# The second merged stage of a recurrent network kernel: routing by pairs of tiles, and the third LSTM 24 steps behind the second

## The reference, cut to what matters

```
hs = LSTM_1(x, h0=cond)            # second LSTM of the kernel: 128 times, one after the other
# experts on hs, for each of 32*128 tokens:
logits = hs @ Wr + br              # 16 experts
w, i = top_2(softmax(logits)); w = w / sum(w)
h = gelu(layernorm(hs @ W1[e] + b1[e]) * g1[e] + be1[e])     # for each expert e
x = x + sum over the 2 chosen e of w_e * (h_e @ W2[e] + b2[e])
h3 = LSTM_2(x, h0=cond)            # third LSTM: goes to the attention of the next stage
# LSTM step: z = x_t @ Wx + b + h @ Wh; c = f*c + i*g; h = o * tanh(c)
```

## Time and profile before

| what | value |
|---|---|
| median of three runs | 4591.94 us |
| the profiled execution | 4592.8 us, its span 4591.0 us |
| mean granted TensorE clock | 0.963 |
| PE busy | 4209.4 us (92%) |
| DVE busy | 2537.7 us (55%) |
| ACT busy | 1904.5 us (41%) |
| POOL busy | 784.3 us (17%) |

### The profile page before, as it was taken

The page is one execution under the profiler, slowest core; times in us unless marked ns, Lnnn a source line. Parts: engine busy times, 40 slices in busy tenths (PEclk is TensorE's granted clock), DMA queues, the critical chain, the costliest instruction groups (busy, mean ns, idle before and its releaser), DMA issues. The chain is left out here.

```text
span 4591.0 us, 117961 instructions
## 1 busy us (share of the span) xinstructions
PE 4209.4 (92%) x40912; PEld 2942.6 (64%) x40912; DVE 2537.7 (55%) x7670; ACT 1904.5 (41%) x4829; POOL 784.3 (17%) x3251
## 2 busy tenths in 40 slices
PE   6999999999998888898799998999996887889998
PEld 4555776887775455554355887887783555566666
DVE  5775564555554888886555445666666554421111
ACT  4343443333332555564233222666663552333333
POOL 1111221000000666663221000111112110000000
PEclk9999999999999999999799998999998998989999
DMA  1000000000000000000000000000000000000000
GB/s 54 0 0 25 0 0 26 1 0 0 0 0 11 1 2 1 1 1 1 34 0 3 0 0 1 3 3 3 3 3 13 41 0 0 0 1 0 0 0 18
DMA packets 3085, 28.94 MB, mean 6 GB/s; under 512 B 320, under 2 KB 832, under 8 KB 1216
## 3 DMA queue, kind: packets, MB, share of 16 engines
q1 hardware_dynamic: 2768, 24.97, 1.4%
HBM read 22.87 MB, written 2.10 MB: 5 GB/s over the span
## 5 line engine op out<-in xcount | busy, mean ns | idle before, releaser
L2312 DVE SCALAR_TENSOR_TENSOR experts_acc<-banks,experts_gate,experts_acc 128x128 f32<-128x128 f32 x512 | 144.2, 344 | 462.1 <-PE banks L2258 461.0
L2258 PEld LDWEIGHTS banks<-weights,experts_hidden 128*128 128x128 f32 x2560 | 303.3, 192 | 55.0 <-issue 49.7
L604 DVE TENSOR_REDUCE cells_row_max<-banks 128x4 f32<-128x512 f32 x384 | 238.5, 684 | 162.8 <-PE banks L397 162.8
L2258 PE MATMUL banks<-weights,experts_hidden 128*128 128x128 f32 x2560 | 305.2, 275 | 0.0
L2531 ACT ACTIVATE experts_hidden<-banks,weights 128x512 f32<-128x512 f32 x256 | 175.9, 687 | 271.1 <-PE banks L2528 267.2
L761 PE MATMUL banks<-clock_fill 128*128 128x512 bf16 x932 | 282.6, 392 | 1.2 <-PEq L101 1.2
L2528 PE MATMUL banks<-act_a,weights 128*128 (+1 forms) x512 | 263.4, 646 | 0.0
L541 ACT ACTIVATE cells_probs<-banks 128x512 f32<-128x512 f32 x384 | 198.3, 602 | 97.4 <-PE banks L437 90.1
L604 DVE TENSOR_REDUCE attn_row_max<-banks 128x4 f32<-128x512 f32 x256 | 159.0, 684 | 133.4 <-PE banks L397 133.4
L1579 ACT ACTIVATE wave_hidden_turned<-banks,weights 128x128 f32<-128x128 f32 x512 | 205.7, 454 | 40.4 <-PE banks L1523 37.3
L2717 ACT ACTIVATE lin_context_turned<-banks 128x256 f32<-128x256 f32 x128 | 49.2, 384 | 403.7 <-PE banks L2669 403.7
(11 more groups left out here) (528 smaller groups left out, 9909.9 us busy)
## 6 DMA issues: line engine op xcount, KB each, us to landing
weights<-in_p SPq DMA_DIRECT2D x1, 2894.5 KB, 17.2
weights<-in_p SPq DMA_DIRECT2D x1, 2894.0 KB, 9.4
weights<-in_p SPq DMA_DIRECT2D x2, 1396.0 KB, 7.6
x_res<-in_x SPq DMA_DIRECT2D x1, 2048.0 KB, 15.2
out_x<-x_res SPq DMA_DIRECT2D x1, 2048.0 KB, 6.3
weights<-in_p SPq DMA_DIRECT2D x1, 1836.0 KB, 10.9
weights<-in_p SPq DMA_DIRECT2D x1, 1835.5 KB, 6.9
weights<-in_p SPq DMA_DIRECT2D x1, 1344.5 KB, 9.6
```

Source lines behind the costliest of these rows:

```text
L604: dve.tensor_reduce(mt[:, 4 * g:4 * g + 4], bank, AX_X, ALU.max).then_inc(s["max_ready"], 1)
L2258: last = pe.matmul(ps[:, 2 + e % 2, t * P:(t + 1) * P], hs[lo:lo + n, (tile + f) % slots, t * P:(t + 1) * P], out_rhs(e, f, lo, n), start= ...
L2312: last = dve.scalar_tensor_tensor(out=acc[:, t, :], in0=ps[:, 2 + e % 2, t * P:(t + 1) * P], scalar=g[:, t, e:e + 1], in1=acc[:, t, :], op ...
```

## The change

It sets WAVE_LAG from 32 to 24, so that the chain has 152 steps in place of 160. It lowers all expert lags but LOGITS by 8: ROUTE and HID from 18 to 10, UNIT 11, TURNED 12, OUTPUT 13, SUM 14, TOTAL 18, GTURN 16, HSRC 6, GSRC 12. To have the logits of a group at step 10, routing works on pairs of tiles: the same 17 instructions and three parts every 8 steps, at steps 10, 11 and 12, then 18, 19 and 20 and so on, on tensors of half the width. The counts of the waits that order the bank SIDE follow. The loop's bounds (44 to 123) and the place of `prepare(0, 4)` (step 12) stay.

```diff
-WAVE_PERIOD, WAVE_LAG, WAVE_FIRST, WAVE_LAST = 16, 32, 44, P - AHEAD
+WAVE_PERIOD, WAVE_LAG, WAVE_FIRST, WAVE_LAST = 16, 24, 44, P - AHEAD
...
-    HID, UNIT, TURNED, OUTPUT, SUM, TOTAL, LOGITS, GTURN, ROUTE = 18, 19, 20, 21, 22, 26, 5, 24, 18
+    HID, UNIT, TURNED, OUTPUT, SUM, TOTAL, LOGITS, GTURN, ROUTE = 10, 11, 12, 13, 14, 18, 5, 16, 10
     STATE, SIDE, HBANK, TURN, OUT = 2, 3, 4, 6, 7
-    HSRC, GSRC, KEPT = 14, 20, WAVE_LAG + AHEAD + 3
-    NEWTON, ROUTING = 11, 16
+    HSRC, GSRC, KEPT = 6, 12, WAVE_LAG + AHEAD + 3
+    NEWTON, ROUTING, PAIR = 11, 16, 2 * AHEAD
...
-        m1, m2, best, dist = (sb(n, [P, 4]) for n in ("first", "second", "best", "distance"))
-        hot1, hot2, work = (sb(n, [P, 4, NE]) for n in ("hot1", "hot2", "work"))
+        m1, m2, best, dist = (sb(n, [P, 2]) for n in ("first", "second", "best", "distance"))
+        hot1, hot2, work = (sb(n, [P, 2, NE]) for n in ("hot1", "hot2", "work"))
...
+        def pair_of(st, lag):
+            return st.i * (WAVE_PERIOD // PAIR) + (st.c - lag) // PAIR
+
         def group_at(st, part, known):
 
             if known and not ROUTE <= st.c - part < ROUTE + P:
                 return None
-            return st.group(ROUTE) if (st.c - ROUTE) % WAVE_PERIOD == part else None
+            return pair_of(st, ROUTE) if (st.c - ROUTE) % PAIR == part else None
...
-                    tile_gates(tile, (st.c - GSRC) // 4 % 2, st.group(GSRC))
+                    tile_gates(tile, (st.c - GSRC) // 4 % 2, pair_of(st, GSRC))
...
-            keep(P - AHEAD, 3)
+            keep(P - AHEAD, ((P + WAVE_LAG) // AHEAD - 1) % 4)
...
-                past(pe, s["gt_ready"], tile - 4)
-                past(pe, s["stored"], tile - 5)
+                past(pe, s["gt_ready"], tile - 2)
+                past(pe, s["stored"], tile - 3)
...
-                pe.wait_ge(s["lg_ready"], tile + 5 if not isinstance(tile, int) or tile + 5 < NB else NB)
+                pe.wait_ge(s["lg_ready"], tile + 3 if not isinstance(tile, int) or tile + 3 < NB else NB)
...
-                pe.wait_ge(s["lg_ready"], tile + 6 if not isinstance(tile, int) or tile + 6 < NB else NB)
+                pe.wait_ge(s["lg_ready"], tile + 4 if not isinstance(tile, int) or tile + 4 < NB else NB)
...
-                part_ = (st.c - ROUTE) % WAVE_PERIOD
+                part_ = (st.c - ROUTE) % PAIR
...
-                values = lg[:, tok(group * 4, 4), :]
+                values = lg[:, tok(group * 2, 2), :]
                 if part_ == 0:
                     if at == 0:
-                        dve.wait_ge(s["lg_ready"], group * 4 + 4)
+                        dve.wait_ge(s["lg_ready"], group * 2 + 2)
...
-                        dve.tensor_scalar(gates[:, tok(group * 4, 4), :], hot1[:, :, :], 0.5, None,
+                        dve.tensor_scalar(gates[:, tok(group * 2, 2), :], hot1[:, :, :], 0.5, None,
```

More of the change, by code:

```diff
@@ L1737, in logits @@
                                   ALU.add).then_inc(s["lg_ready"], 1)
-            over = lambda t: t[:, :].unsqueeze(2).broadcast_to([P, 4, NE])
-            tie = const("tie16").unsqueeze(1).broadcast_to([P, 4, NE])
+            over = lambda t: t[:, :].unsqueeze(2).broadcast_to([P, 2, NE])
+            tie = const("tie16").unsqueeze(1).broadcast_to([P, 2, NE])
             def pick_best(at, values, top, hot, routed):
```

## The result

The changed kernel took 4583.83 us (median of 19 runs, 4576.18 to 4590.47) beside 4592.48 for the kernel before (19 runs): ratio 0.9979 [0.9971, 0.9986], about -9.6 us. Two further measurements of the same kernel gave 0.9969 [0.9958, 0.9979] and 0.9973 [0.9964, 0.9982].

The account below looks back on a forecast made before the run. No engine alone was the bound: PE, DVE and POOL wait in a ring, in a chain of 160 steps each ending at ACT's state write. Five terms summed to -25.7 us, from 4591.94 to 4566, range 4557 to 4576.

Parts of the forecast that it names:

- term 1: Steps 10 to 17, the second LSTM alone with four filler products each, disappear: -31.75 us.
- term 2: DVE's block splitting the third LSTM's weights stays, now at step 12 among expert work: +2.1 us, bounds 0 and 6.5.
- term 3: Eight steps get both LSTMs with experts in place of the third LSTM alone with experts: +0.77 us, bounds 0.3 and 1.5.
- term 5: The eight old routing passes handle 32 in place of 64 elements: -0.2 us, bounds 0 and -3.2.
- rival B: The clock falls again behind the moved block, now under expert steps: 4570.6 us, chance 0.20.
- Term 4: Eight extra routing passes, at step 20, five loop-head steps, and 124 and 132: +3.4 us, bounds 0 and 6.4.
- Rival C: Passes at the loop's first steps cost the full 0.80 and the clock falls each turn: 4575.6 us, chance 0.08.
- Stages behind unchanged within 2 us: Sign expected in the profile after: the stages behind the edited one keep their time within 2 us.
- all three alarms: Signs of being wrong: a four without a pass's end over 19.4, loop-head fours over 21.5, over 10 us at 1.2 GHz in the stage.

Follow-up runs that it names:

- written out: This stage's loop replaced by written-out steps: in the changed kernel 0.9923 and 0.9929 of before, in the kernel before 0.9980.
- pairs alone: The kernel before with routing by pairs of tiles, all lags as before (160 steps), loop kept: ratio 1.0023 to before.
- the filling: The changed kernel with filler products on PE, seven in the loop's first step and two in its second: 0.9969 of before.

## Why the prediction was wrong

The chain can be split by its steps. "Measured" is the mean of three profiles of the changed kernel less that of three of before; "written out" has one profile each.

| steps (of the changed kernel from the second row on) | forecast | measured | written out |
|---|---|---|---|
| 10 to 17 of before, which go (term 1) | -31.75 | -30.1 | -31.75 |
| 10 to 35: the block (term 2) and the pass at 20 | 2.1 + 0.3 | +2.2 | +2.6 |
| 36 to 43, both LSTMs, for 128 to 135 of before (term 3) | +0.77 | +0.2 | +0.3 |
| 44 to 123, the loop: five passes at its first steps | +2.0 | +8.8 | +0.0 |
| from 124 on: two passes | +1.1 | +1.2 | +1.7 |
| term 5 | -0.2 | in the rows above | in the rows above |
| sum | -25.7 | -17.7 | -27.1 |

**Terms 1 to 3** (light steps gone, the moved block, eight steps with both LSTMs) held in the main: 152 states; the table load 26.9 us earlier than the earlier trace rows, or 31.0 counted from the state of step 9, which ran 4.06 later this time. Term 1 was 1.65 too large. I read it from one profile, whose light steps held a clock fall of 10.2 us and took 31.75; in a second profile of before the fall was 3.4 us and they took 29.57, in a third there was none and they took 28.99. I took the fall as caused by the block, but one profile of a clock fall is a draw. Before written out drew 10.2 us again, which is luck for the last column. Term 3 came out just under its lower bound of 0.3. Inside term 2 two details were off. The state behind the block came 5.4 us behind the last, not 6 to 7. And the clock did fall at the start of the expert work in each profile of the changed kernel (3.4 us from 1467.6, 0.89 over 1464 to 1480), but ahead of the block, which began at 1479.6; rival B's mechanism was not what happened.

**Term 4 failed, at its second clause**: five passes at the loop's first steps at 0.4 each, because "part of the pass hides there, since POOL's Newton steps are late already". The heads were late because of DVE's jump, which I had not looked for; a pass there does not hide in that lateness, it delays the jump. Measured: four heads, not five (the loop is entered at step 44 without a jump), at +2.4 each, 9.7 in place of 2.0. That is 7.7 more than forecast. The loop's other steps gave 0.9 of it back; with term 1's 1.65, and 0.4 the other way in the rest, this makes the 8.0 us by which the chain missed.

**Terms 4 and 5 away from the heads.** I had held that a pass on half the width costs nearly what a whole one does. The least time of one instruction (226 ns at 64 elements, 192 at 32) bears that out, the chain does not. Written out, four steps with the end of a group's pass in the loop's range took 19.84 to 20.22 us, with the end of a pair's 19.33 to 19.47 (19.77 in one), without one 19.07 to 19.10 in most: 0.75 to 1.1 for a group, 0.25 to 0.4 for a pair. With the loop the five fours with an old pass fell by 2.8 us in all and those without rose by 1.9, where term 5 took off 0.2. The product with the distance took 360 ns at the median in place of 532, but not by its width. By the rule of the Trainium skill that I had cited ("SBUF — State Buffer", section Who interferes with whom) half the width doesn't shorten the blocked time, and the traces agree: where POOL's copy of the inputs began with the product, it took 530 to 534 ns at 64 elements and 496 to 501 at 32, less by the same 34 that separate the least times of 226 and 192. The 356 to 365 ns came where that copy had begun 0.15 us earlier. Either way the product was held up until some 0.3 us after the copy's start, not for all of the 0.46 us that the profile shows for the copy.

**Rival C** had the right place and, in "the clock falls in each turn", half of the mechanism; I gave it 0.08 because one fall in five heads looked like an accident. Its price, 9.4 above the forecast, is near the 7.7 measured at the heads. Even so its 4575.6 is below the result, because of what follows.

**"Stages behind unchanged within 2 us" failed**: 6.8 us more outside the chain on the mean of three profiles, 5.4 of them behind it and 1.4 ahead. It need not be the work of pairs or lags: before with one turn more written out shows 9 more, and before wholly written out 2 less. The stage with the cells behind it took 725.7 to 726.1 us in before (three profiles) and 734.3, 729.3, 729.4 in the changed kernel, and the difference arises behind the two jumps of that stage's own loop: there the granted clock was at its lower level for 13.6, 6.8 and 10.2 us in before and for 20.4, 17.0 and 13.6 in the changed kernel (20.4 in before with one turn more written out, whose stage took 736.6). Whether where the instructions lie causes it or the moment at which the clock falls there, no run separates; it stays open.

Of my own tests all three alarms rang: a four without a pass's end at 19.48 (over 19.4), heads over 21.5, 13.6 us at 1.2 GHz in the stage (10.2 in the second profile).

## What to carry to other kernels

Ahead of any edit in a hardware loop, find where each engine's jump stands relative to the chain: idle time put down to "issue" at the first step of every turn was the jump here. Work with waits of its own that is added just ahead of it moves the whole gap onto the chain, and shifting the loop by a few steps or writing it out takes it off again. Price a change that touches a loop's head from that head, and a sum of one stage against changes of several us elsewhere that come with any new build.

## What the runs showed of the hardware

- A taken jump of this stage's loop cost DVE 2.8 to 3.1 us to its next instruction in most builds and 3.5 to 3.8 in one, counted from when its sequencer reaches the jump, not from when its work ends. POOL's was similar (2.5 to 3.4), ACT's 0.24. In the loop of the stage with the cells it was ACT's that took 2.5 to 4.0 and POOL's that took 0.3: turns of 415 and more recorded instructions had the long gap on these three engines, turns of 228 to 233 the short one.
- PE idled 1.48 to 1.93 us at each of the twelve heads of the changed kernel's three profiles, and 3.4 us at 1.2 GHz followed at eight; with pairs alone 1.23 to 1.68 us and four of four; with the filling 0.35 to 0.75 and none of four; in before with its loop a turn later 1.27 to 1.51 and one of three. The length of the idle time alone doesn't decide it: 1.48 to 1.59 us passed without a fall at four heads, 1.23 was followed by one. Falls elsewhere moved from one execution to the next of the same kernel.
- The time outside the edited stage was 3854.7 to 3870.1 us over fourteen profiles of nine kernels, all with the same work there, and differed by up to 9 between executions of the changed one (3868.7, 3862.1, 3859.5).
- A DVE product of two inputs in SBUF took 192 ns at 32 elements and 226 at 64 at the least, and 496 to 501 and 530 to 534 when a copy of POOL began with it.
